# Layer 0 of the first sample ahead of all eight weight products, whose results two engines take out

## The reference

```
x = x + L0(x)   # agg_w[b] @ x[b] + agg_b[b]
x = x + L1(x)   # grouped conv, 4 groups, 9 taps, + c_weight @ cond[b] + bias
x = x + L2(x)   # as L0, own weights
x = x + L3(x)   # as L0, own weights
# L0, L2, L3: h = gelu(gelu(cond@W0+b0)@W1+b1); att = softmax(h@W2+b2)   (32 x 8)
#             agg_w[b] = sum_k att[b,k]*weight[k];  agg_b = att @ bias_k
```

## Time and profile before

| | before |
|---|---|
| median of 3 runs | 485.47 us |
| the profiled execution | 484.1 us |
| its span in the trace | 482.3 us |
| PE busy | 473.2 us, 98% |
| PE weight loads busy | 446.3 us, 93% |
| DVE busy | 320.2 us, 66% |
| ACT busy | 248.5 us, 52% |
| POOL busy | 151.2 us, 31% |
| line 508 / 488 / 537 on the chain that ended last | 59% / 18% / 15% |

### The profile page before, as it was taken

The page is one execution under the profiler, slowest core; times in us unless marked ns, Lnnn a source line. Parts: engine busy times, 40 slices in busy tenths (PEclk is TensorE's granted clock), DMA queues, the critical chain, the costliest instruction groups (busy, mean ns, idle before and its releaser), DMA issues.

```text
span 482.3 us, 17714 instructions
## 1 busy us (share of the span) xinstructions
PE 473.2 (98%) x8003; PEld 446.3 (93%) x8003; DVE 320.2 (66%) x409; ACT 248.5 (52%) x414; POOL 151.2 (31%) x151
## 2 busy tenths in 40 slices
PE   8989999999999999999999999999999999999996
PEld 7978999999999999999999999999999999999995
DVE  3548687767676876767687776767777676777424
ACT  5654445466544545654455466444545654455544
POOL 2935072324133322414331331333223142420110
PEclk9999999999999999999999999999999999999998
DMA  8696977676546476664746666464667746452224
GB/s 277 207 334 184 302 232 226 209 221 208 186 120 215 156 217 219 207 216 112 211 149 217 209 214 216 129 206 140 215 203 220 220 149 208 131 187 77 90 88 175
DMA packets 39244, 92.86 MB, mean 193 GB/s; under 512 B 4601, under 2 KB 25473, under 8 KB 35201
## 3 DMA queue, kind: packets, MB, share of 16 engines
q1 hardware_dynamic: 39168, 91.73, 60.5%
HBM read 53.95 MB, written 37.77 MB: 190 GB/s over the span
## 4 chain that ended last, share of the span: by engine, by line
PE 97%; DMA 1%; issue 1%; DVE 0%; SPq 0%; DVEq 0%
PE cv_ps L508 59%; PE aux_ps L488 18%; PE aux_ps L537 15%; PE cv_ps L444 2%; PE cv_ps L431 1%; DMA consts_sb<-in_consts_dram 1%; PE cv_ps L537 1%; PE aux_ps L431 1%; PE aux_ps L466 0%; DVE y_all L847 0%; DVE m_all L797 0%; PE aux_ps L455 0%; PE aux_ps L400 0%; SPq L318 0%; SPq L319 0%
## 5 line engine op out<-in xcount | busy, mean ns | idle before, releaser
L508 PE MATMUL cv_ps<-x_hi,conv_lo 32*128 32x512 f32 x1536 | 284.7, 391 | 0.0
L508 PE MATMUL cv_ps<-x_hi,conv_hi 32*128 32x512 f32 x1536 | 284.2, 389 | 0.0
L508 PE MATMUL cv_ps<-x_lo,conv_hi 32*128 32x512 f32 x1536 | 284.2, 391 | 0.0
L508 PEld LDWEIGHTS cv_ps<-x_lo,conv_hi 32*128 32x128 f32 x1536 | 172.5, 184 | 4.7
L508 PEld LDWEIGHTS cv_ps<-x_hi,conv_hi 32*128 32x128 f32 x1536 | 171.5, 183 | 5.6
L508 PEld LDWEIGHTS cv_ps<-x_hi,conv_lo 32*128 32x128 f32 x1536 | 172.4, 183 | 4.5
L779 DVE SCALAR_TENSOR_TENSOR x_lo<-cv_ps,d_all,x_hi 128x512 fp32r<-128x512 f32 x128 | 87.2, 744 | 132.4 <-ACT x_hi L626 132.4
L636 ACT ACTIVATE y_all<-aux_ps,e_all 128x512 f32<-128x512 f32 x122 | 74.0, 689 | 134.1 <-PE aux_ps L537 134.1
L626 ACT ACTIVATE x_hi<-cv_ps,d_all 128x512 fp32r<-128x512 f32 x128 | 77.5, 688 | 67.9 <-PE cv_ps L508 67.9
L488 PE MATMUL aux_ps<-x_hi,a_hi 32*128 32x512 f32 x512 | 99.5, 391 | 2.3 <-issue 2.3
L488 PE MATMUL aux_ps<-x_hi,a_lo 32*128 32x512 f32 x512 | 99.1, 388 | 0.0
(11 more groups left out here) (104 smaller groups left out, 455.5 us busy)
## 6 DMA issues: line engine op xcount, KB each, us to landing
x_sb<-in_x_dram SPq DMA_DIRECT2D x31, 1024.0 KB, 6.5
out_dram<-y_all SPq DMA_DIRECT2D x60, 512.0 KB, 7.4
a_rep<-a_pairs SPq DMA_DIRECT2D x64, 128.0 KB, 7.3
m_rep<-m_pairs SPq DMA_DIRECT2D x64, 128.0 KB, 6.1
out_dram<-y_all SPq DMA_DIRECT2D x8, 256.0 KB, 2.6
a_pairs<-a_all SPq DMA_DIRECT2D x1, 1920.0 KB, 12.4
m_pairs<-m_all SPq DMA_DIRECT2D x1, 1792.0 KB, 12.2
m_all<-in_mix_dram SPq DMA_DIRECT2D x2, 512.0 KB, 5.5
```

The costliest lines, as they stand in the source:

```text
L508: mm = pe.matmul(cv_ps[:, g, :], w[rows(g), j, :], a[n % 2][rows(g), q, s:s + T], start=(i == 0), stop=(i == steps - 1))
```

## The change

- PE: `bias_e` is no longer in two halves; all of it comes behind the last mixture. Layer 0 of sample 0 comes directly behind it, and then all eight quads without a break. The wait for the last mixtures moves from quad 0 to layer 0. `fill(7)` becomes `fill(8)` and `fill(8)` becomes `fill(12)`.
- Quads' results: ACT takes out the even ones and DVE the odd ones, both behind their `x1_out(0)`. ACT's splits of sample 1 (`split_second_x_hi`) come behind quads 0 and 2, DVE's (`split_x_lo(1, h)`) behind quads 1 and 3. One semaphore becomes two.
- SP: the load of `conv_f` moves from before the small save to behind `replicate_a0(0)`.
- POOL: `split_a0(0)` moves ahead of all work on `conv_f`.

```diff
@@ sync
-            sp.dma_start(conv_f[:], conv).then_inc(conv_loaded, DMA)
             sp.wait_ge(d_ready, 1)
...
             replicate_a0(0, range(PH))
+            sp.dma_start(conv_f[:], conv).then_inc(conv_loaded, DMA)
             load(1)
...
-            sp.wait_ge(m_out, 1)
+            sp.wait_ge(*m_taken(0))
...
-            sp.wait_ge(m_out, B // QUAD)
+            sp.wait_ge(*m_taken(B // QUAD - 2))
+            sp.wait_ge(*m_taken(B // QUAD - 1))
@@ tensor
             def quad_product(m):
-                if m == 0:
-                    pe.wait_ge(*mix_taken(MIXES - 2))
-                    pe.wait_ge(*mix_taken(MIXES - 1))
-                wait(pe, m_out, m + 1 - RING)
+                if RING <= m:
+                    pe.wait_ge(*m_taken(m - RING))
@@ layer0_steps, n == 0 and p == 0
                     pe.wait_ge(e_out, 1)
+                    pe.wait_ge(*mix_taken(MIXES - 2))
+                    pe.wait_ge(*mix_taken(MIXES - 1))
@@ order of TensorE
-            fill(7)
+            fill(8)
...
-            fill(8)
+            fill(12)
...
             biases()
-            in_turn(mixing, 2 * G)
-            bias_e(range(0, 4))
             in_turn(mixing)
-            bias_e(range(4, K)).then_inc(e_made, 1)
-            for m in range(4):
-                quad_product(m)
+            bias_e().then_inc(e_made, 1)
             in_turn([layer0_steps(0, p) for p in range(PH)])
-            for m in range(4, B // QUAD):
+            for m in range(B // QUAD):
                 quad_product(m)
@@ scalar
-            for m in range(3):
-                m_evacuate(m)
-            split_second_x_hi(0)
-            m_evacuate(3)
-            split_second_x_hi(1)
             act.wait_ge(bias_out, 1)
             x1_out(0)
-            for m in range(4, B // QUAD):
+            for m in range(0, B // QUAD, 2):
                 m_evacuate(m)
+                if m // 2 < HALVES:
+                    split_second_x_hi(m // 2)
@@ gpsimd
+            split_a0(0)
             pool.wait_ge(conv_loaded, DMA)
...
-            split_a0(0)
             split_a0(1)
@@ vector
+            def m_evacuate(m):
+                dve.wait_ge(m_made, m + 1)
+                nc.vector.tensor_copy(m_columns(m), prep_ps[m % RING]).then_inc(m_out_v, 1)
...
-            split_x_lo(1, 0)
-            split_x_lo(1, 1)
             dve.wait_ge(bias_out, 1)
             x1_out(0)
+            for m in range(1, B // QUAD, 2):
+                m_evacuate(m)
+                if m // 2 < HALVES:
+                    split_x_lo(1, m // 2)
```

More of the change, by code:

```diff
@@ L216, in cond_resid_kernel @@
         m_made = sem("m_made")
-        m_out = sem("m_out")
+        m_out_a = sem("m_out_a")
+        m_out_v = sem("m_out_v")
         zero_cols = sem("zero_cols")
@@ L253, in mix_taken, with m_taken, m_columns @@
             return mix_out_a if BY_SCALAR[t] else mix_out_v, sum(by == BY_SCALAR[t] for by in BY_SCALAR[:t + 1])
+        def m_taken(m):
+            return (m_out_v if m % 2 else m_out_a), m // 2 + 1
+        def m_columns(m):
+            return m_all[:, QUAD * m:QUAD * (m + 1), :].rearrange("p n m -> p (n m)")
         h_ps = [[cv_ps[:, h, 0:REPEAT * B]] + [aux_ps[:, 2 * h + n, 0:REPEAT * B] for n in range(NL - 1)] for h in range(2)]
@@ L457, in biases, with bias_e @@
                 pe.matmul(c2_ps, bias_sb[:, 1, :], att_t[:, 1, :], start=True, stop=True).then_inc(c_made, 1)
[L459 to L465, removed]
+            def bias_e():
+                pe.wait_ge(e_loaded, DMA)
+                pe.wait_ge(c2_att_ready, 1)
+                for n in range(1, NL):
+                    pe.matmul(e_ps, bias_sb[:, n, :], att_t[:, n, :], start=(n == 1), stop=False)
+                for k in range(K):
                     mm = pe.matmul(e_ps, w3_sb[:, k, :], c2_att[:, k, :], start=False, stop=(k == K - 1))
@@ L499, in conv_steps @@
                     pe.wait_ge(zero_cols, 4)
-                    pe.wait_ge(m_out, B // QUAD)
+                    pe.wait_ge(*m_taken(B // QUAD - 2))
+                    pe.wait_ge(*m_taken(B // QUAD - 1))
                 if g == 0:
@@ L640, in m_evacuate @@
                 act.wait_ge(m_made, m + 1)
-                nc.scalar.activation(m_all[:, QUAD * m:QUAD * (m + 1), :].rearrange("p n m -> p (n m)"),
-                                     prep_ps[m % RING], ACT.Identity).then_inc(m_out, 1)
+                nc.scalar.activation(m_columns(m), prep_ps[m % RING], ACT.Identity).then_inc(m_out_a, 1)
             for t in range(MIXES):
```

## The result

The changed kernel takes 486.77 us (median of 13 runs, 485.78 to 488.10) against 485.05 us (13 runs, 484.02 to 485.97): a ratio of 1.0046 with a 95% interval of 1.0036 to 1.0056, or some 2.2 us (the two medians by themselves lie 1.7 us apart). The profiled execution took 486.59 us, its span is 484.8: 2.5 more than before. I had forecast 0.2 more. The time lies in the stated range, and 0.46% lies just inside the 0.5% that I had called no change. But the interval excludes a ratio of 1: with this many runs the kernel is measurably slower.

A forecast was written before the change was run, and what follows sets the result against it. TensorE was taken to bound the main part. Layer 0's start at 22.7 less 22.52 gave +0.2 us on 484.1, hence 484.3, or 485.6 as a median; all other terms nothing. Range 483.8 to 488.1.

The forecast's parts named there:

- What bounds the kernel: Main part: TensorE bounds it, busy 473.2 of 482.3 us, so only when it gets there matters.
- T0: Start of layer 0 of sample 0 on TensorE, forecast at 22.7 us; the lanes begin 11.09 us later.
- Why the save was late: Small save to DRAM: held by the 768 KB of conv_f ahead of it; without them 2.6 us instead of 4.4.
- Rival 2: Save and copies of a0 land no sooner: lanes 2.0 to 2.6 us late, 487.5 to 488.1 median; chance 0.12.
- The hole moves and doesn't close: TensorE's wait for a0 moves from 24.1 to about 20.4 us and is as long as it was.
- Layer 0 costs 3.48 us as before: Layer 0 of sample 0 on TensorE: 3.48 us, within 11.09 us of work up to the lanes, before and after.
- Nothing is lost in the quads: Eight quads behind layer 0 of sample 0: results taken out in time, 0.7 us or more to spare, no stalls.
- T: End of layer 0 of sample 0, forecast at T0 + 3.48 = 26.2 us.
- What is late next: Loads and splits behind the a0 copies: conv_f lands at 24.3, split of sample 1 done at 32.1, hidden by 1.7 us.
- Rival 3: VectorE's low part of x and GpSimd's split of sample 1 block each other: 1.2 us, 486.8; chance 0.17.
- The fills: Five more fill matmuls on TensorE, one at the start and four later: priced at nothing.

The follow-up runs named there:

- filled hole: The changed kernel with 18 matmuls of zeros on TensorE between bias_e and layer 0 of sample 0: 484.63 us, ratio 1.0005.
- the long hole: The kernel before the change with three memsets on GpSimd ahead of its split of a0 of sample 0: 486.60 us, ratio 1.0048.
- the last of four arrangements of loads and splits: The kernel before with the change's SyncE and GpSimd edits and fills, both a0 splits first, x of sample 1 loaded ahead of conv_f: 483.00 us, ratio 0.9974.

## Why the prediction was right or wrong

- **What bounds the kernel, and T0.** Right. I gave 16.1 for the landing of the small save, 20.6 for the copies, 22.6 for the split and 22.7 for layer 0. The chain shows 13.51 + 2.36 = 15.87, 20.34, 22.35 and 22.60.
- **Why the save was late.** Right: with `conv_f` out of the way it took 2.4 us instead of 4.4, and 1.7 to 2.5 in the other profiles of kernels with this edit. Rival 2 is out.
- **The hole moves and doesn't close.** Right, and a bit longer than said: 2.7 us from 19.9, since PE was done 0.4 earlier.
- **Layer 0 costs 3.48 us as before.** This is the step that failed: "From the end of all mixtures and biases to the lanes it has 3.84 + 3.48 + 3.77 = 11.09 us of work, before and after". The work is the same, its time isn't: 5.92 us at a granted clock of 0.50, which is 2.44 of the 2.5 us by which the lanes are late. The filled hole shows that this is the loss: 1.0005 instead of 1.0046. The row that I quoted for the hole carried a clock of 1.00, and I took the clock for a property of the kernel instead of asking what the new hole would do to it. None of my rivals had it. That the time still lies in the range is luck: the range reached up to 488.1 for rival 2, which didn't come.
- **Nothing is lost in the quads.** Right that none stalls: 7.58 us for eight in one block. The sum's 7.61 was a little too much: where the clock was back, eight quads took 7.34 (the filled hole), and some 0.24 of the 7.58 went to the first 0.4 us at the low clock. ACT began on quad 0 at 30.53 and DVE on quad 1 at 31.67, 2.0 and 3.2 us behind T; I had 2.3 and 3.4.
- **What is late next.** Right that nothing was. GpSimd of the changed kernel, and below it VectorE:

```profile
23.25 0.83 POOL L724 TENSOR_TENSOR conv_f<-conv_f,consts_sb 128x32 f32<-128x32 f32 x4 [0.91 <-DMA conv_f<-in_conv_dram]
...
29.78 1.27 POOL L699 TENSOR_TENSOR a_lo<-a_rep,a_hi 128x512 fp32r<-128x512 f32 x1
```

```profile
31.67 0.68 DVE L751 COPY m_all<-cv_ps 128x512 f32<-128x512 f32 x1
32.27 1.22 DVE L758 TENSOR_TENSOR x_lo<-x_sb,x_hi 128x1024 fp32r<-128x1024 f32 x1
```

`conv_f` landed at 23.2 (I had 24.3), the split of sample 1 was done at 31.05 (32.1), and TensorE has no wait from 28.5 on.

- **Rival 3.** It didn't come here, and that was luck: GpSimd was done at 31.05 and VectorE's low parts of x began at 32.27, 1.22 us each, but only because layer 0 was 2.44 us late. At the forecast's 3.48 they would have begun at about 29.8 (an estimate from these rows), inside the split. With the hole filled they did meet: the first low part, at 30.64, took 1.50 us, and nothing waited for it. So the price of 1.2 us was too high for this order. With SyncE's and GpSimd's edits alone the meeting cost 1.9 us on the split.
- **The fills.** I had them at nothing. On the kernel before they cost 0.25%, and the lack of them costs the changed kernel another 0.4%. In the profiled executions both losses show falls of the clock.

What stays open: what decides whether the clock falls in a given hole. Falls were seen 2.3 us behind PE's last work (the changed kernel), and 5.0 us behind it (the long hole), and right behind a hole of 2.1 us, where the profile of the kernel before kept its clock behind 2.26. Even profiles of kernels that are the same up to that point differ in whether and where it falls. That the fills cost the kernel before their 0.25% through this fall fits one profile and the mean clocks, and was not tested; why longer fills at 6 us should do so is open.

## What to carry to other kernels

A hole in TensorE that is moved isn't worth the same in its new place: ask of each hole what the granted clock was behind it, and price the work behind it at the lower clock as well: here layer 0 took 1.4 to 1.7 times its 3.48 us. In the one wait where it was tried, matmuls of zeros that ended before the wait did cost nothing that shows and kept the clock. If they outlast the wait, they delay what follows: with the slow fills attention began at 9.70 instead of 8.44. And where a load and its splits are moved, follow each engine that reads the same landing: the hole closed in full only in the last of four arrangements of loads and splits, and 1.3 us of its 2.3 were had.

## What the runs showed of the hardware that was not expected

The granted clock fell in or up to 1.0 us behind holes of 2.1 to 4.1 us, and behind holes of 0.8 to 1.2 us after the second fill (at 8.9, 9.3 and 9.4, in three profiles with the old fills). The stretches at 0.50 lasted 3.4 or 6.8 us, most of it with TensorE at work. The Trainium skill ("TensorE: Matmul & The Clock Gate", What's actually happening) has the two levels, 1.2 and 2.4 GHz, and idle time as what leads to the lower; the fall to 0.50 in the hole and layer 0's 5.92 us against 3.48, all of it at the lower level, agree with that.

The row of the granted clock doesn't tell everything at the start of a program. The first fill of the changed kernel, at 1.19, shows 8 matmuls in 2.08 us, 0.26 each, against 12 in 1.70, 0.14 each, for its second fill; the clock stands at 1.00 for both.

The save of 128 KB to DRAM took 1.7 to 2.5 us in the profiles of kernels that load the 768 KB of `conv_f` later (2.4 in the changed kernel), and 4.4 behind them in the kernel before. The four copies took 4.5 us both in the kernel before and in the changed one, though issuing them took 2.61 us before and 1.76 after; in the other profiles of kernels that load `conv_f` later they took from 4.6 to 5.9.
